# Residuals made early, two query products moved and half of the mixing first, in a kernel of conditioned mixing, attention and feed-forward

## What is computed

```python
x = x + attn(cond(x, cond_128))         # x: 64 x 32 x 512, f32
x = x + ffn(cond2(x, cond_128))
# cond:  att = softmax(gelu(gelu(c @ W0 + b0) @ W1 + b1) @ W2 + b2)         64 x 8
#        y[b] = sum_k att[b,k] weight[k] @ x[b] + att[b] @ bias_k           mixes the 32 rows of x[b]
# attn:  q = y @ Wq, k and v = y @ Wkv, 32 heads of 16 over 8 groups of k and v, causal softmax over
#        32 rows, ctx @ Wo + bo
# cond2: convolution of 9 taps along 512, 4 groups, plus a shift from c
# ffn:   (silu(h w1) * (h w3)) w2, each with a low-rank term of rank 16 folded into its weight
```

## Time and profile before

| what | us |
| --- | --- |
| median of 3 runs | 638.76 (638.19 to 640.67) |
| the profiled execution | 639.44 |
| its span | 637.40 |
| PE busy | 605.8 (95%) |
| DVE, ACT, POOL busy | 236.4, 164.3, 154.3 |
| projections, attention, feed-forward | from about 18, 110 and 233 |

### The profile page before, as it was taken

The page is one execution under the profiler, slowest core; times in us unless marked ns, Lnnn a source line. Parts: engine busy times, 40 slices in busy tenths (PEclk is TensorE's granted clock), DMA queues, the critical chain, the costliest instruction groups (busy, mean ns, idle before and its releaser), DMA issues.

```text
span 637.4 us, 8134 instructions
## 1 busy us (share of the span) xinstructions
PE 605.8 (95%) x3274; PEld 498.6 (78%) x3274; DVE 236.4 (37%) x342; ACT 164.3 (26%) x278; POOL 154.3 (24%) x107
## 2 busy tenths in 40 slices
PE   5899999389998999999999999999999999999997
PEld 4788888277776888888798888888888879888885
DVE  1434335779999463111143111124211115211112
ACT  3461332344433043333211111111111111111110
POOL 2430010698898654444200000000000000000000
PEclk9999999769999999999999999999999999999999
DMA  7991313634585370000007000003500000300001
GB/s 231 380 406 39 132 66 84 218 91 125 160 203 173 132 165 2 0 1 1 0 2 198 0 1 0 1 1 95 102 0 0 0 0 0 133 0 1 1 1 66
DMA packets 34509, 51.13 MB, mean 80 GB/s; under 512 B 11153, under 2 KB 19729, under 8 KB 33233
## 3 DMA queue, kind: packets, MB, share of 16 engines
q1 hardware_dynamic: 34192, 49.43, 25.2%
q10 hardware_dynamic: 288, 1.31, 0.5%
HBM read 37.08 MB, written 12.60 MB: 78 GB/s over the span
## 4 chain that ended last, share of the span: by engine, by line
PE 82%; DVE 11%; POOL 3%; issue 2%; ACT 1%; DMA 0%; ACTq 0%; DVEq 0%; POOLq 0%
PE twin L1124 38%; PE twin L1145 19%; PE twin L1008 9%; PE twin L1022 7%; PE twin L984 2%; DVE total L824 2%; DVE probs L818 2%; DVE probs_t L839 2%; PE twin L1091 2%; PE twin L995 2%; POOL probs L543 1%; DVE rows L855 1%; PE twin L947 1%; DVE ctx_lo L845 1%; PE twin L968 1%
## 5 line engine op out<-in xcount | busy, mean ns | idle before, releaser
L903 DVE TENSOR_TENSOR gate<-twin,gate 128x512 f32<-128x512 f32 (+1 forms) x44 | 30.4, 691 | 255.5 <-PE twin L1124 255.5
L1124 PE MATMUL twin<-c_hi,f_hi 128*128 128x512 f32 (+1 forms) x352 | 96.0, 394 | 0.6 <-DVE c_lo L874 0.6
L1124 PE MATMUL twin<-c_hi,f_lo 128*128 128x512 f32 (+1 forms) x352 | 96.3, 395 | 0.0
L1124 PE MATMUL twin<-c_lo,f_hi 128*128 128x512 f32 (+1 forms) x352 | 95.7, 393 | 0.0
L1124 PEld LDWEIGHTS twin<-c_hi,f_lo 128*128 128x128 f32 (+1 forms) x352 | 65.7, 187 | 16.5
L1124 PEld LDWEIGHTS twin<-c_hi,f_hi 128*128 128x128 f32 (+1 forms) x352 | 65.2, 185 | 17.0 <-issue 1.0
L1124 PEld LDWEIGHTS twin<-c_lo,f_hi 128*128 128x128 f32 (+1 forms) x352 | 65.3, 185 | 16.1
L1145 PE MATMUL twin<-f_lo,gate_hi 128*128 128x512 f32 (+1 forms) x176 | 69.5, 395 | 0.0
L726 ACT ACTIVATE gate<-twin 128x512 f32<-128x512 f32 (+1 forms) x44 | 26.4, 600 | 165.9 <-PE twin L1124 165.9
L729 ACT CAST gate_hi<-gate 128x512 fp32r<-128x512 f32 (+1 forms) x44 | 27.3, 620 | 128.2 <-DVE gate L903 128.2
L1145 PE MATMUL twin<-f_hi_head,gate_hi 128*128 128x512 f32 x128 | 50.7, 396 | 0.0
(11 more groups left out here) (131 smaller groups left out, 800.4 us busy)
## 6 DMA issues: line engine op xcount, KB each, us to landing
f_sb<-in_f SPq DMA_DIRECT2D x2, 2752.0 KB, 20.2
x_sb<-in_x SPq DMA_DIRECT2D x16, 256.0 KB, 2.9
q_t<-q_dram SPq DMA_DIRECT2D x8, 512.0 KB, 4.2
x_dram<-rows SPq DMA_DIRECT2D x16, 256.0 KB, 3.0
near<-x_dram SPq DMA_DIRECT2D x16, 256.0 KB, 6.6
rows<-x_dram SPq DMA_DIRECT2D x4, 1024.0 KB, 5.9
out<-rows SPq DMA_DIRECT2D x16, 256.0 KB, 2.1
f_sb<-in_f SPq DMA_DIRECT2D x1, 2560.0 KB, 10.0
```

The source lines that it names most:

```text
L903: dve.tensor_tensor(gate[0:w, h % 2, :], up_bank[2 * (h % 2) + 1][0:w, :], gate[0:w, h % 2, :], ALU.mult).then_inc(gate_ready, 1)
L1124: mm = pe.matmul(bank[0:w, :], f[:, c, :], c_part[:, c, :], start=(n == 0 and c == 0), stop=(n == 2 and c == DC - 1))
```

## The change

1. **Mixing by halves.** PE makes the mixing of the first 32 sequences (`make_mix(0)`, products of 128 columns) before the projections, and that of the others behind the value product of the first block. att_diag is one DVE operation with a mask `own_row`. The shifts of the first block are broadcast by a product on PE (`shift_rows`, `ones_rows`) and a copy by ACT instead of a DMA. Four products on zeros (`keep_clock`) stand in PE's order. The loop over the blocks is written out on PE and DVE.
2. **Splits later.** ACT rounds wq between the y_hi of the first block, and POOL starts to take wq_lo when y_lo of that block is done.
3. **Residuals in the projections.** POOL makes x + bo of blocks 0 and 1 after the y_lo of the second block and of blocks 2 and 3 after that of the third, into three stages. SP stores them to x1 in HBM. In attention SP reloads them into `rows` four tiles ahead. The loads of x for blocks 2 and 3 stand behind the stores in SP's order.
4. **The add moved.** ACT copies each output product out of PSUM (`out_stage`), and POOL adds it to the residual at the end of its iteration. SP's store of x1 waits for that (`x1_ready`), and so does ACT's split of f1 after attention.
5. **Two query products moved.** Of the last block, Q2 and Q3 are made after scores 0 and 1 of attention (LATE_Q = 2). All 16 folds now come before scores 0. SP stores that block's queries in iteration 2.
6. wo is loaded and split before attention; the broadcast convb_all moves from the opening to iteration 4.

The diff, cut to its core:

```diff
+STAGES = 3
+RESID_PHASES = ((), (0, 1), (2, 3), ())
+LATE_Q = 2
...
-            made = ps[n][:, :].rearrange("p (o t c) -> p t o c", o=8, c=BT)
-            return copy(mix[c * S:(c + 1) * S, :, c, n * 8:(n + 1) * 8], made[c * S:(c + 1) * S, :, :, c])
+            half, part = n // 2, n % 2
+            made = ps[n][:, :].rearrange("p (o t c) -> p t o c", o=16, c=BT)
+            return copy(mix[c * S:(c + 1) * S, half * 8:(half + 1) * 8, c, part * 16:(part + 1) * 16],
+                        made[c * S:(c + 1) * S, :, :, c])
...
-            sp.dma_start(mixb_all[:, 0:BLOCK], mix_shifts[:, 0:BLOCK].to_broadcast([P, BLOCK]))\
-                .then_inc(mix_shift_spread[0], 16)
...
+            def store_resid(blk):
+
+                for tile in range(blk * TILES, (blk + 1) * TILES):
+                    sp.wait_ge(resid_ready, tile + 1)
+                    sp.dma_start(x1_rows[:, tile, :], resid_stage[:, tile % STAGES, :])\
+                        .then_inc(resid_stored[tile % STAGES], 16)
+
+            def load_resid(tile):
+
+                sp.wait_ge(resid_stored[tile % STAGES], 16 * (tile // STAGES + 1))
                 if tile >= TILES:
 
-                    sp.wait_ge(resid_ready, tile - TILES + 1)
-                sp.dma_start(x_sb[:, tile % TILES, :], x_rows[:, tile, :]).then_inc(x_reloaded[tile % TILES], 16)
+                    sp.wait_ge(x1_stored[tile % TILES], 16 * (tile // TILES))
+                sp.dma_start(rows[:, tile % TILES, :], x1_rows[:, tile, :]).then_inc(resid_loaded[tile % TILES], 16)
...
             for i in range(BLOCKS):
-                if i + 2 < BLOCKS:
-
+                if i == BLOCKS - 1:
+
+                    sp.wait_ge(front_filled, (BLOCKS - 2) * USES + DC)
+                    sp.dma_start(wo_sb[:, :, :], wo).then_inc(wo_loaded, 16)
                     sp.wait_ge(front_filled, i * USES + DC)
-                    sp.dma_start((x_sb, rows)[i % 2][:, :, :], x_rows[:, (i + 2) * TILES:(i + 3) * TILES, :])\
-                        .then_inc(x_loaded[i % 2], 16)
-                if i == BLOCKS - 1:
+                    for tile in range(TILES):
+                        load_resid(tile)
 
                     sp.wait_ge(front_emptied[1], i * (USES // 2) + emptied(DC + 1) + 1)
                     sp.wait_ge(q_stored[0], 16 * BLOCKS // 2)
-                    sp.wait_ge(zeros_set, 4)
+                    sp.wait_ge(zeros_set, 3)
                     for g in range(2):
                         queries_and_keys(g)
-                if i == BLOCKS - 2:
...
+                for blk in RESID_PHASES[i]:
+                    store_resid(blk)
+                    if blk + 2 < BLOCKS:
+
+                        sp.wait_ge(front_filled, blk * USES + DC)
+                        sp.dma_start((x_sb, rows)[blk % 2][:, :, :], x_rows[:, (blk + 2) * TILES:(blk + 3) * TILES, :])\
+                            .then_inc(x_loaded[blk % 2], 16)
+                if i < BLOCKS - 1:
+                    store_queries(i)
 
...
-                sp.wait_ge(front_emptied[t % 2], emptied(PROJECTED + tile) + 1)
+                sp.wait_ge(x1_ready, tile + 1)
                 sp.dma_start(x1_rows[:, tile, :], rows[:, t, :]).then_inc(x1_stored[t], 16)
...
                     store_x1(n - OUT - 1)
+                if due(n, OUT + 2) and n - OUT - 2 + TILES < QUADS:
+                    load_resid(n - OUT - 2 + TILES)
+                if n == 2:
+                    store_queries(BLOCKS - 1)
+                if n == 2 * BLOCKS + 2:
+                    sp.wait_ge(q_stored[1], 16 * BLOCKS // 2)
                 if n % 2 == 0 and 2 <= n // 2 + 1 < 2 * BLOCKS:
                     queries_and_keys(n // 2 + 1)
-                if TILES <= n + 1 < QUADS:
-                    reload_x(n + 1)
+                if n == TILES:
+
+                    sp.wait_ge(conv_shift_stored, 16)
+                    sp.wait_ge(front_filled, PROJECTED)
+                    sp.dma_start(convb_all[:, :], shifts_dram[0:1].rearrange("m b s -> m (b s)").to_broadcast([P, N]))\
+                        .then_inc(conv_shift_spread, 16)
...
+            pool.wait_ge(y_lo_ready, DC)
...
+            for i, phase in enumerate(RESID_PHASES):
+                pool.wait_ge(y_lo_ready, (i + 1) * DC)
+                for tile in [blk * TILES + t for blk in phase for t in range(TILES)]:
+                    blk, t = divmod(tile, TILES)
+                    pool.wait_ge(x_loaded[blk % 2], 16 * (blk // 2 + 1))
+                    if tile >= STAGES:
+                        pool.wait_ge(resid_stored[tile % STAGES], 16 * (tile // STAGES))
+                    pool.tensor_tensor(resid_stage[:, tile % STAGES, :].rearrange("p (r n) -> p r n", r=BT),
+                                       (x_sb, rows)[blk % 2][:, t, :].rearrange("p (n r) -> p r n", r=BT),
+                                       bo_all[:, :].rearrange("p (r n) -> p r n", r=BT), ALU.add)\
+                        .then_inc(resid_ready, 1)
+
...
+            pool.wait_ge(front_filled, (BLOCKS - 1) * USES + DC + 1)
             pool.memset(v_wide[:, :, :, :, :], 0.0).then_inc(v_cleared, 1)
-
-            pool.wait_ge(bo_spread, 16)
+            for j in range(REP):
+                pool.wait_ge(wo_hi_split, j + 1)
+                pool.tensor_tensor(wo_lo[:, j, :], wo_sb[:, j, :], wo_hi[:, j, :].bitcast(F32),
...
-                if due(n, RESID):
-
-                    i, t = divmod(n - RESID, TILES)
-                    pool.wait_ge(x_reloaded[t], (i + 1) * 16)
-                    if i:
-                        pool.wait_ge(x1_stored[t], i * 16)
-                    pool.tensor_tensor(rows[:, t, :].rearrange("p (r n) -> p r n", r=BT),
-                                       x_sb[:, t, :].rearrange("p (n r) -> p r n", r=BT),
-                                       bo_all[:, :].rearrange("p (r n) -> p r n", r=BT), ALU.add)\
-                        .then_inc(resid_ready, 1)
-                if n == QUADS + RESID - 1:
+                if due(n, OUT):
+
+                    tile = n - OUT
+                    t = tile % TILES
+                    pool.wait_ge(front_emptied[tile % 2], emptied(PROJECTED + tile) + 1)
+                    pool.wait_ge(resid_loaded[t], 16 * (tile // TILES + 1))
+                    pool.tensor_tensor(rows[:, t, :], out_stage[:, tile % 2, :], rows[:, t, :], ALU.add)\
+                        .then_inc(x1_ready, 1)
+                if n == QUADS:
...
+            act.wait_ge(first_shift_filled, 1)
+            act.copy(mixb_all[:, 0:BLOCK], ps[4][:, :]).then_inc(mix_shift_spread[0], 16)
...
+                        if blk == 0:
+
+                            act.wait_ge(wq_loaded, 16)
+                            act.copy(wkq_hi[:, 1 + c, :, :], wq_sb[:, :, c, :]).then_inc(wkq_hi_split, 1)
...
+                if due(n, OUT):
+
+                    tile = n - OUT
+                    act.wait_ge(front_filled, PROJECTED + tile + 1)
+                    if tile == 0:
+
+                        act.wait_ge(q_stored[1], 16 * BLOCKS // 2)
+                    if tile >= 2:
+                        act.wait_ge(x1_ready, tile - 1)
+                    act.copy(out_stage[:, tile % 2, :], front[tile % 2][:, :])\
+                        .then_inc(front_emptied[tile % 2], 1)
...
-            act.wait_ge(resid_ready, BLOCKS * TILES)
+            act.wait_ge(x1_ready, BLOCKS * TILES)
...
-            for c in range(BT):
-                dve.tensor_copy(att_diag[c * S:c * S + K, c, :], ps[3][c * S:c * S + K, 0:B]).then_inc(cond_dve, 1)
-
-            dve.wait_ge(zeros_set, 3)
-            for n in range(4):
+            dve.wait_ge(own_row_set, 1 + BT)
+            dve.tensor_tensor(att_diag[:, :, :], ps[3][:, 0:B].unsqueeze(1).to_broadcast([P, BT, B]),
+                              own_row[:, :].unsqueeze(2).to_broadcast([P, BT, B]), ALU.mult).then_inc(cond_dve, 1)
+            dve.wait_ge(cond_dve, 4)
+            dve.wait_ge(mix_loaded, 16)
+            dve.tensor_tensor(shift_rows[:, :, :], att_diag[0:K, 0, 0:BB].unsqueeze(2).to_broadcast([K, BB, S]),
+                              param("mix_b", K).unsqueeze(1).to_broadcast([K, BB, S]), ALU.mult)\
+                .then_inc(shift_rows_ready, 1)
+
...
-                if due(n, OUT):
-
-                    tile = n - OUT
-                    t = tile % TILES
-                    dve.wait_ge(front_filled, PROJECTED + tile + 1)
-                    dve.wait_ge(resid_ready, tile + 1)
-                    dve.tensor_tensor(rows[:, t, :], front[t % 2][:, :], rows[:, t, :], ALU.add)\
-                        .then_inc(front_emptied[t % 2], 1)
...
+            def keep_clock(times):
+
+                for _ in range(times):
+                    pe.matmul(ps[7][:, :], mask_rows[:, :, :].rearrange("p g k -> p (g k)"),
+                              mask_rows[:, :, :].rearrange("p g k -> p (g k)").unsqueeze(1).to_broadcast([P, BT, P]),
+                              start=True, stop=True)
+
+            pe.wait_ge(mask_set, 1)
```

(24 more changed lines are left out.)

210 lines of the change are left out of this document (112 added, 98 removed).

## The result

The changed kernel takes 642.44 us (641.68 to 644.43, 7 runs), the kernel before 638.76 (637.97 to 640.67, 7 runs): a ratio of 1.0055, 95% interval 1.0041 to 1.0069. The forecast was 634.2 in a range of 629.0 to 640.5, so both the time and the sign were wrong. The profiled execution took 644.08 for a span of 642.3. The same kernel, profiled a second time beside the experiments, took 643.04 for a span of 641.2; 5 runs of it had a median of 644.60, ratio 1.0077 (1.0050 to 1.0103). I use both profiles, since they differ in the opening.

What follows compares the result with a forecast made beforehand. PE was taken to carry the span, with DVE full in attention's steady part. Opening -2.5, folds -2.2, filling -1.0, steady +1.4, end -1.2, join +0.3 made -5.2 against 639.44: 634.2 us, range 629 to 640.5.

Steps and rivals of the forecast that it cites:

- The opening: Start up to the first key product: 23.7 instead of 26.17, 2.5 us earlier (1.7 to 3.1).
- The last folds to scores 0: Stretch before attention without the two query products: 4.8 instead of 6.9, gain 2.1, scores 0 at 105.1.
- The third block's x: Load of x behind four residual stores, costed at nothing; a rival had it 2 late, 636, chance 0.30 shared with another.
- DVE is no longer the bound: Steady part of attention: DVE loses an add of 0.6 from its full 5.91, leaving 5.3 an iteration.
- The loop through SP: Steady part: odd scores to those three later 18.1 through POOL's add, SP's issues and loads; four iterations take 23.4.
- every second iteration from 8 on: Sign in the profile that the forecast is right: PE's scores held by a DMA at these iterations of attention.
- third rival: Steady part: the clock falls in PE's pauses of about 2.7 before even iterations from 8; 9 slower, 643, chance 0.10.
- the last clause of the steady part: Scores 5 to 15: 59.5 instead of 58.1, 1.4 more, with the last loads late beside the near loads.
- The filling: Scores 0 to scores 5: context 0 at 122.0, scores 5 at 133.5, 5.7 earlier in all, 1.0 of it here.
- second rival: Waits after Q1 bring the lower rate for scores 0 and both query products: 638, chance 0.30 shared with late x.
- The end: End of attention: DVE's chain behind scores 15 loses two adds, -1.2; ACT's split of f1 at the join costs 0.3.

Runs made afterwards that it cites:

- e9: Changed kernel with POOL's add of a finished tile moved ahead of its multiplication by the inverse: 638.07 us, ratio to before 0.9986.
- e3: Changed kernel with the four loads of near rows (1 MB) moved from iteration 10 to 14 of SP's loop: 636.46 us, ratio to before 0.9958.
- e2: Changed kernel with only the reload of the residual moved behind the queries and keys in SP's order: 639.71 us, ratio to before 1.0009.
- e1: Changed kernel with queries and keys issued ahead of the store of x1 and the reload in SP's order: 632.03 us, ratio to before 0.9894.
- e5: e1 with LATE_Q = 0, both query products back in the projections: 632.69 us, ratio to before 0.9898.
- e12: e11 with LATE_Q = 0 and 38 idle products behind scores 3 in place of 8 and 22: 629.26 us, ratio to before 0.9854.
- e4: Changed kernel with the second half of the mixing made right behind the shift product: 643.31 us, ratio to before 1.0060.
- e7: e1 plus products nobody reads, 8 behind the last folds and 22 behind scores 3: 629.46 us, ratio to before 0.9836.
- e11: e7 with the near loads in iteration 12 and idle products in three more pauses: 628.98 us, ratio to before 0.9844.

## Why the prediction was wrong

**What held.** The opening in seven of the ten profiled executions with the halved mixing and the zero products: 23.08 to 23.73, forecast 23.7. The other three had 26.81 to 27.01, later than the kernel before, which lies outside the gain of 1.7 to 3.1 that was given. The last folds to scores 0: 104.61 to 104.93 against 105.1. The third block's x was never late. DVE is no longer the bound: a turn of 5.33. The loop through SP, 18.1 from odd scores to those three later: from scores 9 at 160.52 to scores 12 at 178.56 it is 18.04, and without the multiplication's 1.9 in it (e9) no pause is left there.

The loop also says where the pauses come. It spans three turns, and the next odd scores follow 5.3 behind, so by the forecast's own sum PE waits once in four iterations, ahead of scores 8 and 12. There they came. The sign "at every second iteration from 8 on" and the third rival's four pauses didn't follow from that sum.

**The step that failed** is the last clause of the steady part: "1.4 more, the last loads late beside the near loads". The sum took each load at its usual landing (7.3 from q_t's issue), and priced the 1 MB of near rows in the same queue with part of 1.4. It costs 5 to 5.5 (e3 against the two profiles), in three steps:

- In the kernel before, q_t was issued 4.9 behind the near loads too, and took 6.1 to land instead of 3.7 to 4.2, but it went out early enough to hide that. Now the store behind the near loads took 6.23 to land, and the reload waited 4.1 for it in SP's order, ahead of the queries. Where the reload was taken out of the way (e2), q_t itself took 9.0.
- That made a pause of 4.1 at PE, 3 more than without the near loads.
- In it the clock fell, which made the next turn 7.75 instead of 5.34, another 2.4.

I had looked at which wait SP's order puts ahead of the queries (the add's), and not at the second wait that the change puts there: the reload's, for the landing of a store.

Second, the sum had no fall of the clock in the steady part at all. Besides the one at scores 14 there was one at scores 8 in four of the five profiles with a pause of 2.0 to 2.45 there, 1.6 more. That e3 took 60.0 where 59.5 was forecast is therefore in part luck: 1.6 of the 60.0 are this fall, which the forecast didn't have, and without it the loop would have come to 58.4.

Here the Trainium skill, "DMA: Bandwidth & Descriptors", says in "Issuing engines are not separate DMA queues" that transfers run on the same 16 DMA engines and interleave, whichever engine starts them. The trace agrees as far as it goes: behind the near loads q_t took 6.1 before, 9.0 in e2 and 8.4 in e1 (where it was early enough to hide it), and 3.7 to 5.3 elsewhere in the steady part. No run issued them from another engine.

**The third rival** named the fall of the clock in such pauses and gave 643, and 642.44 was measured. It had a chance of 0.10. Its argument against, that the clock had never fallen from 140 to 200, came from pauses of 0.6. The long pause of the trace, 9.89 ahead of context 0, had brought the lower rate; of those between, the rows had 1.30 ahead of the mixing of x, with 4.10 for the mixing and so no fall. The pauses of 2.0 to 4.1 lay between 1.30 and 9.89, where no row said anything, and I counted them with the 0.6. The rival had four falls at 4 each; there were one or two, at 2.4 and 1.6, and a pause of 4.1 that it didn't have. That its price was right is luck: two wrong sizes cancelled.

**The filling** was forecast 1.5 too early at context 0 (122.0; 123.25 to 123.53 measured) and 1.1 at scores 5. The second rival's first half was true as well: the clock fell behind the pause of 2.0 ahead of scores 0, and Q2, in most profiles scores 0 too, ran at the lower rate (e1's scores 0 took 1.90 for 1.05). e5 and e12 show what that did: it took back the 1.7 to 2.2 of the moved query products.

**The end.** From scores 15 to the products up 34.9 was forecast. The kernel before has 35.8, and the profiles have 35.3 to 35.9: of the 0.9 half came or nothing. The products up then began at the lower rate in the changed kernel (the first four 2.04; 1.16 before), behind pauses of 1.08 and 0.66. This was not foreseen, and costs 1.4: from there to the end 405.8 against 404.4. e3, e5 and e9 have pauses as long and no fall, so the pauses alone don't decide it.

Of the opening the Trainium skill, "TensorE: Matmul & The Clock Gate", Part 1, says that the point at which the rate rises depends on where in a free-running rhythm the first products land, and puts the variation at half a microsecond either way. The profiles agree that it varies, and differ in the size: with the same instructions PE was at its higher rate by 13.3 in one profile and still at the lower at 20 in the other, the mixing of x taking 4.06 or 6.65. One such opening is 3.3 at the first key product; at scores 5, 1.6 of it was left between the two profiles, and 1.1 in their spans.

**The sum, closed** with the second profile against before: opening -2.5, to scores 0 -2.4, to context 0 +2.2, to scores 5 -1.8, steady +7.4, to the products up -0.5, lower rate there +1.4: together +3.8, span 641.2 against 637.4. Against the forecast's span of 632.2 it is 9.0 more: 6.0 in the steady part, 1.1 up to scores 5, 0.5 at the end of attention and 1.4 behind it.

## What to carry to other kernels

When a change moves the producer of a store later, list everything that the issuing engine has queued behind that store, and for each transfer behind a large one take its landing as measured beside it, not the usual one. Loads that the pipeline will need stand first in such a queue: the same transfers in another order gave 10 us here, and nothing in the kernel whose bound lay elsewhere. Write down which iterations such a loop holds up: that, and not the mean turn, says how long the pauses are. A pause of TensorE is priced with what it does to the rate behind it, and work that is taken out of a pause may leave the pause to the clock and gain nothing.

## What the runs showed of the hardware

- The same opening had its dense products (the mixing of x) at 4.06 or at 6.5 to 6.7 us in different executions, with nothing in the program changed, and the first key product 3.3 later. Not all of that reached the end: the two profiles of the changed kernel differ by 1.1 in span. The granted clock of the page reads full in both, from the first slice on; the durations tell them apart.
- The length of a pause did not tell whether the rate would fall. Ahead of scores 8 it fell behind 2.00 to 2.31 (second profile, e2, e3, e4) and not behind 2.45 (first profile); ahead of scores 12 it did not fall behind 1.36 to 1.98 in any of these. Behind 3.8 to 4.2 ahead of scores 14 it fell in all five profiles that had such a pause.
- Products whose results nobody reads kept the rate in the pauses that they filled: the context product behind one of 6 us took 1.09 instead of 1.98 (e7), and 30 such products made the kernel 2.6 us faster than e1. With 18 more (e11) the whole profile was at full clock, for another 0.5 that the intervals don't confirm.
- Behind 1 MB of near rows, with two stores and a reload of 256 KB each between, a transfer of 512 KB took 9.0 us to land (e2), and 3.7 to 5.3 elsewhere in the steady part; a store of 256 KB took 6.2 in the changed kernel, where the page has 2.1 for the median of such stores.
